# A mixture-of-experts stage that fetches its rows through small records, with a freer order of its additions

## The reference

```python
xn = _layernorm(x, axis=-1)
x = x + _L0_gnn_ref(xn, src, dst, edge_weight, ...) + _L0_mix_ref(xn[None], ...)[0]
x = x + _L0_ffn_ref(_layernorm(x, axis=-1)[None], ...)[0]
```

```python
logits = jnp.einsum('bsd,de->bse', xn, Wr) + br
top_vals, top_idx = jax.lax.top_k(logits, K)          # K = 2
for e in range(E):                                    # E = 8, H = 512
    h = jax.nn.gelu(jnp.einsum('bsd,dh->bsh', xn, W1[e]) + b1[e], approximate=False)
    y_e = jnp.einsum('bsh,hd->bsd', h, W2[e]) + b2[e]
    y = y + y_e * w_full[..., e, None]
```

## Time and profile before

| | |
|---|---|
| median of 3 runs | 4447.44 us (4443.28 to 4449.68) |
| profiled execution: its time, its span | 4440.3 us, 4438.6 us |
| setup and edges | 0 to some 3260 us |
| routing, with plan and fill | 3261 to 3647 us |
| experts | 3647 to 4438.6 us |
| busy: PE, DVE, ACT, POOL | 76%, 56%, 38%, 70% of the span |

### The profile page before, as it was taken

The page is one execution under the profiler, slowest core; times in us unless marked ns, Lnnn a source line. Parts: engine busy times, 40 slices in busy tenths (PEclk is TensorE's granted clock), DMA queues, the critical chain, the costliest instruction groups (busy, mean ns, idle before and its releaser), DMA issues. The chain is left out here.

```text
span 4438.6 us, 85552 instructions
## 1 busy us (share of the span) xinstructions
PE 3389.3 (76%) x16628; PEld 2802.7 (63%) x16629; DVE 2495.7 (56%) x11386; ACT 1685.6 (38%) x3095; POOL 3111.7 (70%) x2088
## 2 busy tenths in 40 slices
PE   1466666667677677878888888888758859999998
PEld 1355555555565555666666666666557758888887
DVE  3577777665555555666666666666548862222222
ACT  1233333344444443444444444444312224444443
POOL 0488888888888888888888888888855544444444
PEclk7788878788888888888888888888779979999999
DMA  9888888877777777777777777777789965565554
GB/s 380 241 146 155 152 148 147 157 117 118 116 109 115 116 113 114 102 108 108 105 104 107 108 103 105 108 107 102 91 217 296 294 187 143 139 145 141 141 140 114
DMA packets 588869, 638.95 MB, mean 144 GB/s; under 512 B 60524, under 2 KB 553156, under 8 KB 587138
## 3 DMA queue, kind: packets, MB, share of 16 engines
q0 software_dynamic: 279264, 269.84, 48.5%
q1 hardware_dynamic: 262234, 273.19, 20.9%
q10 hardware_dynamic: 47304, 95.18, 5.9%
HBM read 249.82 MB, written 390.09 MB: 144 GB/s over the span
## 5 line engine op out<-in xcount | busy, mean ns | idle before, releaser
L818 POOL DMA_INDIRECT agg<-msg,sidx x1664 | 2585.7, 1554 | 667.5 <-issue 408.7
L1122 PE MATMUL bank<-rows,Cmat 128*128 x3328 | 1025.7, 450 | 166.7 <-ACT msg L1315 140.6
L1315 ACT COPY msg<-bank 128x512 f32<-128x512 f32 x832 | 487.1, 585 | 1486.0 <-DMA agg<-msg,sidx 1209.8
L1122 PEld LDWEIGHTS bank<-rows,Cmat 128*128 128x128 f32 x3328 | 699.1, 224 | 346.7 <-issue 253.8
L873 DVE SCALAR_TENSOR_TENSOR sidx<-seen_sum,trash,srcf 128x4 int32<-128x4 f32 x416 | 92.7, 223 | 1022.8 <-DMA agg<-msg,sidx 1017.6
L2069 POOL DMA_INDIRECT out_dram<-x_y,x_node x210 | 325.7, 1551 | 473.1 <-issue 228.2
L856 DVE TENSOR_SCALAR Emat<-bank,srcf,wtf 128x128 f32<-128x128 f32 x1664 | 564.5, 398 | 0.0
L1106 PEld LDWEIGHTS bank<-Emat,pick 128*128 128x128 f32 x3328 | 518.3, 226 | 41.6 <-issue 17.7
L1106 PE MATMUL bank<-Emat,pick 128*128 128x128 f32 x3328 | 528.7, 311 | 1.6 <-DVE seen L860 1.6
L1097 PE MATMUL bank<-packed,both 128*128 (+1 forms) x416 | 187.3, 451 | 437.9 <-DVE seen L860 427.9
L860 DVE SCALAR_TENSOR_TENSOR seen<-bank,srcf,prior 128x128 f32<-128x128 f32 x1664 | 479.1, 341 | 0.0
(11 more groups left out here) (245 smaller groups left out, 4130.6 us busy)
## 6 DMA issues: line engine op xcount, KB each, us to landing
x_w<-in_L_ffn_W_dram SPq DMA_DIRECT2D x105, 512.0 KB, 4.1
agg<-expert_rows ACTq DMA_DIRECT2D x12, 4224.0 KB, 63.3
r_agg<-agg SPq DMA_DIRECT2D x196, 256.0 KB
x_zin<-table SPq DMA_DIRECT2D x105, 259.0 KB, 4.1
window_raw<-in_x_dram SPq DMA_DIRECT2D x208, 128.0 KB, 2.5
agg<-msg,sidx POOLq DMA_INDIRECT x1664
xn_rows<-n_xn ACTq DMA_DIRECT2D x49, 256.0 KB
xn_turned<-n_xnT ACTq DMA_DIRECT2D x49, 256.0 KB
```

What stands on the lines that cost most here:

```text
L818: pool.indirect_dma_start(scratch["agg"][r][:, :], bass.IndirectOffsetOnAxis(ap=sidx[:, j:j + 1], axis=0), msg[:, j % (2 * BATCH), :], Non ...
L1122: mm = nc.tensor.matmul(M[p][:, (q % 2) * D:(q % 2 + 1) * D], Cmat[:, b % 2, q, :], rows[:, bass.ds(slot, 1), :], start=True, stop=True)
L1315: nc.scalar.copy(msg[:, at:at + 2, :].rearrange("p q c -> p (q c)"), M[p][:, :]).then_inc(s_msg, 1)
```

## The change

1. The table holds records of 5 words (node, first choice, lead, mean, 1/deviation), not rows of 259. Routing no longer normalises rows: the mean and the scale are folded into the router weights and the logit step, PE turns x1 itself, and ACT copies in one instruction. The record tile has eight slots (`TURN`), so DVE waits for scatters of eight pairs ago, not four.
2. Routing stores x1 into its own HBM array. The output is set to zero earlier, by 25 DMAs of up to 512 KB that ACT issues in the first 25 groups of the edge phase; the residual is added in the expert phase, by the block of the row's first choice.
3. In the experts, ACT loads the records of block q+3 after the GELUs of q; DVE copies the node numbers out (`tell`); POOL gathers the rows of x1 by two indirect DMAs; DVE normalises them (`normalise`) and forms the residual (`x_residual`). Four slots.
4. POOL waits for the additions of the block before only where its expert differs (`hold`, made in `plan`); otherwise only for those of two and more blocks ago.

```diff
+REC = 5
+NODE, FIRST, LEAD, MEAN, RSTD = range(REC)
...
+TURN = 2 * DEPTH
...
+            def blank_out(n):
+                if isinstance(n, int) and n == DOUBLES - 1:
+                    left = N - n * BLANK * P
+                    act.dma_start(out[N - left:N, :].rearrange("(p a) d -> p (a d)", a=2),
+                                  blank[0:left // 2, 0:2 * D]).then_inc(s_blankout, 16)
+                else:
+                    act.dma_start(out[bass.ds(n * BLANK * P, BLANK * P), :].rearrange("(p a) d -> p (a d)", a=BLANK),
+                                  blank).then_inc(s_blankout, 16)
...
+            sp.wait_ge(s_blankout, 16 * DOUBLES)
             load_expert(7)
...
-                    sp.dma_start(pair_of(out, i), x1[:, u % 2]).then_inc(s_x1st[u % 2], 16)
+                sp.dma_start(pair_of(scratch["x1"], i), x1[:, u % 2]).then_inc(s_x1st[u % 2], 16)
...
-                                                z[:, u, c, :], None).then_inc(s_sent[c][m], 16)
+                                                rec[:, u, c, :], None).then_inc(s_sent[c][m], 16)
...
+                if not below(i, TURN):
+                    for c in range(2):
+                        for m in range(2):
+                            dve.wait_ge(s_sent[c][m], 16 * (i - TURN + 1))
...
-            def normalise(i, u):
+                nc.vector.tensor_scalar(vs[:, s], rec[:, u, :, RSTD], 1.0 + EPS, EPS * EPS, ALU.mult, ALU.add).then_inc(s_st, 1)
+
+            def scale(i, u):
                 s = u % 2
                 dve.wait_ge(s_std, i + 1)
-                nc.vector.reciprocal(scl[:, s], std[:, s]).then_inc(s_scl, 1)
-                dve.wait_ge(s_scl, i + 1)
-                if not below(i, DEPTH):
-                    dve.wait_ge(s_T, i - DEPTH + 1)
-                    for c in range(2):
-                        for m in range(2):
-                            dve.wait_ge(s_sent[c][m], 16 * (i - DEPTH + 1))
-                nc.vector.tensor_copy(z[:, u, :, D], nodes[:, bass.ds(2 * i, 2)])
-                for c in range(2):
-                    last = nc.vector.tensor_scalar(z[:, u, c, 0:D], x1[:, s, c, :], mv[:, s, c, 0:1], scl[:, s, c:c + 1],
-                                                   ALU.subtract, ALU.mult)
-                last.then_inc(s_z, 1)
+                nc.vector.reciprocal(rec[:, u, :, RSTD], std[:, s]).then_inc(s_scl, 1)
+                nc.vector.tensor_copy(rec[:, u, :, NODE], nodes[:, bass.ds(2 * i, 2)])
 
             def route(i, u):
                 logit = L[u % 2].rearrange("p (a e) -> p a e", a=2)
                 dve.wait_ge(s_L, i + 1)
-                nc.vector.tensor_tensor(lg[:], logit, br[:].rearrange("p (a e) -> p a e", a=1).to_broadcast([P, 2, NE]),
-                                        ALU.add).then_inc(s_lg, 1)
+                dve.wait_ge(s_scl, i + 1)
+                for c in range(2):
+                    last = nc.vector.scalar_tensor_tensor(out=lg[:, c, :], in0=logit[:, c, :], scalar=rec[:, u, c, RSTD:RSTD + 1],
+                                                          in1=brc[:], op0=ALU.mult, op1=ALU.add)
+                last.then_inc(s_lg, 1)
...
+                     nc.vector.tensor_tensor(alike[:, 1:BLOCKS], pe_[:, 1:BLOCKS], pe_[:, 0:BLOCKS - 1], ALU.is_equal))
+                step(nc.vector.scalar_tensor_tensor(out=hold[:, 1:BLOCKS], in0=alike[:, 1:BLOCKS], scalar=-16.0,
+                                                    in1=landed[:, 2:BLOCKS + 1], op0=ALU.mult, op1=ALU.add))
...
-                pe.wait_ge(s_z, i + 1)
+                pe.wait_ge(s_sum, i + 1)
...
-                for a in range(HALF):
-                    last = nc.scalar.activation(xf[:, s, a, :], T[s][:, a * D:(a + 1) * D], ACT.Identity,
-                                                bias=beta[:, a:a + 1], scale=gamma[:, a:a + 1])
-                last.then_inc(s_xf, 1)
+                nc.scalar.copy(xf[:, s].rearrange("p a c -> p (a c)"), T[s][:, :]).then_inc(s_xf, 1)
...
-                if not first(k):
-                    sp.wait_ge(s_T, q - 1)
-                    sp.nop(nofuse=True)
-                    sp.wait_ge(s_share, q - 1)
-                    sp.nop(nofuse=True)
-                sp.dma_start(zin[:, s], scratch["table"][bass.ds(at, CAP), :].rearrange("(a p) d -> p a d", p=P)).then_inc(s_z[s], 16)
...
-                pe.wait_ge(s_z[s], 16 * k + 16)
...
+                pe.wait_ge(s_zn, q + 1)
...
+            def load_records(k, u):
+                at = act.value_load(offset[0:1, bass.ds(SLOTS * k + u, 1)], min_val=0, max_val=TABLE_ROWS - CAP)
+                act.dma_start(rec[:, u], scratch["table"][bass.ds(at, CAP), :].rearrange("(p a) d -> p a d", p=P)
+                             ).then_inc(s_rec[u], 16)
...
+                if not over(q + AHEAD):
+                    if not below(q, 1):
+                        act.wait_ge(s_share, q)
+                        act.nop(nofuse=True)
+                    load_records(*ahead(k, u, AHEAD))
+                if not over(q + 1):
+                    features(q + 1, 1 - s)
...
+            def tell(k, u):
+                dve.wait_ge(s_rec[u], 16 * k + 16)
+                nc.vector.tensor_copy(rows[:, u], rec[:, u, :, NODE]).then_inc(s_row, 1)
+
+            def normalise(k, u):
+                q, s = SLOTS * k + u, u % 2
+                dve.wait_ge(s_gat[u], 32 * k + 32)
+                if not below(q, 2):
+                    dve.wait_ge(s_T, q - 1)
+                for c in range(2):
+                    last = nc.vector.tensor_scalar(zn[:, s, c, :], xg[:, u, c, :], rec[:, u, c, MEAN:MEAN + 1],
+                                                   rec[:, u, c, RSTD:RSTD + 1], ALU.subtract, ALU.mult)
+                last.then_inc(s_zn, 1)
+
+            def shares(k, u):
...
+                nc.vector.tensor_scalar(own[:, s], rec[:, u, :, FIRST], iota8[:, bass.ds(e, 1)], None, ALU.is_equal)
...
+                for c in range(2):
+                    last = nc.vector.tensor_scalar(xe[:, s, c, :], xg[:, u, c, :], own[:, s, c:c + 1], None, ALU.mult)
+                last.then_inc(s_xe, 1)
+
+            def finish(k, u):
+                q, s = SLOTS * k + u, u % 2
+                e = expert_of(dve, q)
...
+                dve.wait_ge(s_xe, q + 1)
+                for c in range(2):
+                    nc.vector.scalar_tensor_tensor(out=y[:, s, c, :], in0=y[:, s, c, :], scalar=share[:, s, c:c + 1],
+                                                   in1=xe[:, s, c, :], op0=ALU.mult, op1=ALU.add).then_inc(s_y, 1)
+
+            def body(k, u):
+                q = SLOTS * k + u
+                if not over(q + 1):
+                    normalise(*ahead(k, u, 1))
+                if not over(q + AHEAD):
+                    tell(*ahead(k, u, AHEAD))
+                shares(k, u)
+                finish(k, u)
+
...
-            def body(k, s):
-                q = 2 * k + s
-                for c in range(2):
-                    if s == 1:
-                        pool.wait_ge(s_add[0][c], 16 * k + 16)
-                    elif not first(k):
-                        pool.wait_ge(s_add[1][c], 16 * k)
+            def gather(k, u):
+                pool.wait_ge(s_row, SLOTS * k + u + 1)
                 pool.nop(nofuse=True)
+                for c in range(2):
+                    pool.indirect_dma_start(xg[:, u, c, :], None, scratch["x1"][0:NPAD, :],
+                                            bass.IndirectOffsetOnAxis(ap=rows[:, u, c:c + 1], axis=0)).then_inc(s_gat[u], 16)
+
+            def body(k, u):
+                q, s = SLOTS * k + u, u % 2
+                if not over(q + AHEAD):
+                    gather(*ahead(k, u, AHEAD))
+                if not below(q, 1):
+                    if below(q, 4):
+                        before_landed = 16 * ((q + 1) // 2)
+                    else:
+                        before_landed = pool.value_load(hold[0:1, bass.ds(q, 1)], min_val=16, max_val=16 * (BLOCKS + 1) // 2)
+                    for c in range(2):
+                        pool.wait_ge(s_add[1 - s][c], before_landed)
+                    pool.nop(nofuse=True)
+                if not below(q, 2):
+                    for c in range(2):
+                        pool.wait_ge(s_add[s][c], 16 * (2 * k + u // 2))
+                    pool.nop(nofuse=True)
                 for c in range(2):
```

268 lines of the change are left out of this document (154 added, 114 removed).

## The result

The changed kernel takes **4615.39 us** in the median, the kernel before 4446.15 beside it: ratio **1.0375** [1.0361, 1.039], slower by 169 us; forecast were 4413. Of the four executions one took 12,870 us, which the median counts and the ratio leaves out; the other three took 4610.53 to 4616.27. The profiled execution took 4614.51 us, its span is 4612.8, 174.2 more than before (4438.6).

| part | before | after | |
|---|---|---|---|
| up to the first x1 | 3275.08 | 3274.36 | -0.7 |
| routing, 48 pairs | 336.3 (7.005 a pair) | 361.4 (**7.53**) | +25.1 |
| last x1 to first H | 42.8 | 42.6 | -0.2 |
| experts | 784.5 | **934.5** | +150.0 |

What follows compares the result with a forecast made beforehand. POOL bounds the edge phase and PE the experts; in routing several engines are near their limits. Terms -41 - 3 + 4 + 5 + 1 = -34 us against the median 4447.4 gave 4413 us, range 4387 to 4475.

Steps and rivals of the forecast that it cites:

- Experts, the new chain: Experts: record load, node copy, gather and normalisation reach PE 0.07 us late, shared by two blocks; +5 us with jitter.
- rival 1: Experts: the record lands late and PE waits, making the kernel slower; 4474 us at 3.7 us landing, chance 0.18.
- Landing L = 2.5: Experts: a 5 KB record load lands 2.5 us after issue; 2.0 would cost 0, 4.1 would cost 87 us.
- Register load and issue 0.5: Experts: from the last GELU's start at 3.75 us, register load and DMA issue take 0.5 us, 0.31 of it register load.
- Routing: Routing: DVE's shorter list of 5.94 us plus 0.2 gives 6.15 us a pair instead of 7.005; -41 us.
- Rival 2: Routing: small records cost DMA engines as much as long rows, so 6.6 us a pair and 4435 us; chance 0.13.
- End of routing: End of routing: filler DMAs shrink to 5 KB and POOL's last scatters wait less; -3 us, between 0 and -6.
- start of the experts: Start of experts: record load, node copy, gather and normalisation take 8.2 us where one load took 4.1; +4 us.
- Edges: Edge phase: 25 stores that clear the output are hidden by DMA slack; +1 us, without slack up to +37.
- rival 4: Edge phase: clearing the output isn't hidden, +37 us at most, 4449 us; chance 0.04.
- rival 3: Experts: POOL becomes the bound, through gathers at the additions' price and wakes, 6 to 97 us more; chance 0.10.
- Experts, PE: Experts: PE's products and turns stay the same, at best 105 times 7.34 us, so the change can only lose.

Runs made afterwards that it cites:

- x4_no_w1: r1_turn4 with weight W1 loaded in the first two blocks only, so later blocks multiply by wrong weights: 4496.0 us, ratio 1.0113.
- t3_rec16_turn8: Changed kernel with records of 16 words (64 B) and the record load ahead of the GELUs, still loops of 8 turns: 4401.0 us, ratio 0.9916.
- r2_before8: Kernel before with only its routing loops written out to 8 turns: 4457.5 us, ratio 1.0025.
- r1_turn4: Changed kernel with routing loops of 4 turns and four record slots, as before the change: 4607.7 us, ratio 1.0358.
- s2_rec16: x1_early with records of 16 words (64 B) in place of 5: 4401.5 us, ratio 0.9920.
- t2_after_rec16: Changed kernel with only records of 16 words in place of 5, loops of 8 turns and late record load kept: 4616.2 us, ratio 1.0363.
- s1_pitch128: x1_early with the record tile in SBUF 128 words wide, scatters still sending 20 B a row: 4421.5 us, ratio 0.9963.
- x1_early: r1_turn4 with ACT issuing the record load of block q+3 ahead of the GELUs of q, not behind them: 4449.9 us, ratio 1.0003.
- r8_rec128: x1_early with records of 128 words (512 B) in place of 5: 4406.7 us, ratio 0.9931.
- r5: r1_turn4 with record load ahead of the GELUs, expert node copy behind the results, and ACT copying node numbers into records in routing: 4474.0 us, ratio 1.0053.
- r6: x1_early with DVE taking the place of pair i-2's rows ahead of the 128x1024 addition in routing: 4454.0 us, ratio 1.0038.
- t1: x1_early with an unused SBUF tile behind the records, so later tiles lie as in s1_pitch128: 4450.7 us, ratio 0.9995.

## Why the prediction was wrong

**Experts, the new chain (+5 us forecast, +150 measured): the step that failed most.** The mechanism was rival 1, and its rule held: lateness hits every second block. Of the terms:
- *Landing L = 2.5.* It was 4.0. I had both prices, 2.5 from 1 KB rows beside POOL's additions and 4.1 from the load beside the weights, and put the difference down to the 259 KB of the latter. x4_no_w1 shows that it was the neighbour: 1.9 us to the copy without it, 4.0 behind the 512 KB that SP issues at 4002.97, 0.6 us earlier. My sentence that the load is issued just when the weights are in flight stood under the rival, and should have set the term. By my own formula L = 4.1 gave +87, more than any other term of the sum.
- *Register load and issue 0.5.* 3999.00 + 3.75 is the last GELU, as forecast, and the issue comes at 4003.56, 0.81 later. DVE's register load (0.31 from the earlier trace rows) showed as 0.83 here and 73.9 us in 100 times over the phase. Behind the wait for the record the gap is thus more than twice that of the earlier trace rows; that the load of the earlier trace rows could be started ahead is the likely reason, and not shown.
- *Copy to PE:* 4.01 us by my sum, 4.74 measured, most of it that register load.
- Together PE is 2.0 us late in the round shown, where the copy came 3.5 us after the issue, and (934.5 - 784.5) / 52 rounds = 2.9 in the mean. With the landing at its 4.0 my terms give 0.07 + 1.5 + 0.31 + 0.73 = 2.6 a round, 136 us.

The Trainium skill (DMA: Bandwidth & Descriptors, Anatomy of one DMA) gives a fit that comes to 2.0 us for 5 KB. It is measured on POOL's path, and I used it for a load from ACT's queue. The 1.9 us of x4_no_w1 agree with it, the 4.0 us of the changed kernel don't: the fit has no term for a large load in flight. The Trainium skill (the same page, Latency and other measured facts) has a floor of about 0.6 us for a register load; DVE's gap of 0.74 us in the mean of 100 agrees, and the 0.31 of the earlier trace rows lies below it.

**Routing (-41 forecast, +25 measured): "Between 5.94 and 7.0 I take 6.15".** The list of work was about right: in t3_rec16_turn8, without its two loop returns (12.1 and 12.6 us), the mean of the other 46 pairs is (306.6 - 24.7) / 46 = 6.13 us. The step that failed is the 0.2 us for all that lies beside the lists. Missing were three costs:
- *Longer loops*, 10 us in r2_before8, and 8 us of the kernel between r1_turn4 and the changed kernel. I costed TURN by its slots alone. From 3360 to 3595 the kernel before and r1_turn4, with loops of 4 turns, have no packet of the instruction queues; the changed kernel has 22, three of them at the return shown above (3514 to 3523):

```profile
q14 instruction: 3, 0.02, 1.9%
```

  The Trainium skill (Runtime: NRT & Kernel Launch, Instruction fetch mechanics) says that a taken branch out of the instruction window forces a fetch. The trace agrees: a pair at such a return is 5 to 9 us longer than its neighbours. Against the loops stand the slots: in t3_rec16_turn8 both together cost nothing (6.39 us a pair, 6.40 in s2_rec16), as DVE waits 3.3 us for scatters of earlier pairs there, and 17.7 with four slots.
- *The stops*, up to 65 us (t2 to t3). No row of before could show them, since in that execution no update came late. How much of the 65 the removed normalisation used to cover isn't shown; r2_before8, which has it, stops for 8.1 us, and r1_turn4 and its kin for 20 to 32.
- *20 B scatters*, 20 us (s1 to s2). Rival 2 had this as engine time, and by that measure it is dead: 1.7% of the engines. What grows is the time to land. The Trainium skill (DMA: Bandwidth & Descriptors, Specifications) puts the bound for the full rate at 512 B. For the time of this kernel 64 B are as good as 512; the rate itself no run here tests, with so little to move.

**End of routing** and **start of the experts**: -3 and +4, measured together -0.2. **Edges** +1, measured -0.7: hidden, rival 4 is dead. **POOL** (rival 3): a gather costs 1.00 us, as a scatter, so this rival is dead. **Experts, PE**, "it can only lose": right within 3 us, x1_early needs 781.5 where before needed 784.5.

With the record load moved, 64 B records and an occasion without late updates the kernel takes 4401 us beside 4438, 37 us less, where the sum had -34. That the sums are so close is partly luck: by the traces routing gave 30 of the 41 us, the experts became 3 us shorter where +5 stood, and the stretch up to the first x1 5 us shorter where +1 stood.

## What to carry to other kernels

Price a small load by what is in flight when it is issued, not by its size, and ask first what stands behind its landing on an in-order engine: moving the load by one place, or the copy by one, gave back 141 to 158 us. Compare only kernels that were timed side by side: of the 43 us between x1_early and r8_rec128 some 28 belong to the occasion (4449.9 to 4421.5 of s1_pitch128, as far as that can stand for x1_early). And where a wait has no named releaser, look when its semaphore was updated: here both engines had done their part, and three runs (r5, r6, t1) sought the cause in the kernel, where it wasn't.

## What the hardware did that I had not expected

A loop of 8 turns costs 5 to 9 us at each return, one of 4 turns about 1. On some occasions a tenth of the semaphore updates in routing come 0.3 us late or more, on others none, on the same chip. And after a short idle time of PE its clock can fall. The granted clock in r1_turn4, microsecond by microsecond (the columns of the earlier trace rows):

```profile
3459.00:3460.00 1.00, 0.46 (x4) 0.46 (x5) 0.63 (x3) 0.00 (x0) 0.96 (x1) 1.00 0.83 229
3460.00:3461.00 1.00, 1.00 (x10) 1.00 (x9) 0.00 (x0) 0.00 (x0) 0.32 (x1) 0.75 0.77 137
3461.00:3462.00 1.00, 1.00 (x6) 1.00 (x6) 0.89 (x7) 0.00 (x0) 0.00 (x0) 0.50 0.92 189
```

PE was idle 0.79 us ahead of 3459.54. About 1 us after it had gone on, the clock fell to 0.50, the lower of its two levels (1.2 GHz), and stayed there until some 3463.9; sum_turned took 2.93 us, where it took 2.05 in the earlier trace rows. The mean from 3290 to 3560 is 0.87 in t2_after_rec16, with its stops, and 0.97 in t3_rec16_turn8, without. So a part of the 65 us is likely this; no run separates it.
